# Hop 3 with its slabs 1 and 3 in another pair of PSUM banks

## The chip, the cores and the metric

One core of a Trainium2 chip runs the whole program in one launch. The metric is the device time of that launch in microseconds (us), the median of several runs. A core has five engines with an instruction queue each: TensorE (PE in the profile, with its weight loads as PEld), VectorE (DVE), ScalarE (ACT), GpSimd (POOL) and SyncE (SP, which here only issues DMAs). They wait for each other through semaphores. Matmuls write into PSUM, which has eight banks of 128 partitions by 512 float32; the other engines read the sums from there.

## The reference

The program computes two layers on a graph of 3125 nodes with 256 features and 53125 edges. The part that the change touches is the first neighbour sum of the second layer, and what runs beside it is that layer's linear attention:

```python
xn = _layernorm(x, axis=-1)
x = x + _L1_gnn_ref(xn, edge_index, ...) + _L1_mix_ref(xn[None], ...)[0]

def _gin_agg(h, src, dst, eps, n_nodes):                       # in _L1_gnn_ref
    agg = jax.ops.segment_sum(h[src], dst, num_segments=n_nodes)
    return (1.0 + eps) * h + agg
h = _gin_agg(x, src, dst, eps1, n)          # hop 3, 256 features
h = relu(relu(h @ W1a + b1a) @ W1b + b1b)
h = _gin_agg(h, src, dst, eps2, n)          # hop 4, 512 features

qkv = rmsnorm(x, g_pre) @ w_qkv              # in _L1_mix_ref
q = jax.nn.softmax(q, axis=-2) * SCALE       # within each of 4 heads of 32
k = jax.nn.softmax(k, axis=-1)               # over all nodes
out = einsum(context(k, v), q) @ w_out + b_out, then rmsnorm
```

## The kernel before

Nodes lie in 25 tiles of 128. The features of the stream are also held transposed in `AS` (called `AT`: features on the partitions, nodes along the free axis). The edges are sorted by destination, so the neighbour sum of hop 3 is written as a product with a dense matrix of edge counts. That matrix is built in the first two hops and kept in HBM as `adjacency`, in eight **slabs** of 408 destinations each. A slab has rows for all 3125 sources. It is loaded in five **pieces** of five source tiles, so there are 40 pieces, in a ring of four buffers (two in `onehot`, two in `WA`). SP loads piece i as soon as piece i-4 has been used.

`dense_products` (on PE) goes through the 40 pieces. For each piece and each half `c` of the 256 features it issues 15 matmuls of 128x408 (5 tiles, times 3 bf16 parts into which the float32 features are split: `rows`, and two in `NN`). All 75 matmuls of a slab and a half add up in one PSUM bank, `EDGE[c]`. The last matmul of a slab's half 0 counts up `slab_half`, the last of half 1 counts up `piece_used`, as each piece does.

`dense_sums` (on DVE) goes through the same 40 pieces. Behind the last piece of a slab it reads the slab's first column from a register load (`slab_base`) and adds bank `EDGE[c]` into the 408 columns of `AT` (line 1960), half 0 and then half 1, each add counting up `dense_added`. At the first piece of the next slab PE waits until the add of the same half is done (line 1076), since the slabs share the banks.

Both functions carry side work, held in two tables that are both named `beside_pieces`, from piece 3 on. On PE that is for node tile t: `queries_keys_values(t)` (line 1005, one matmul for each half, behind the 15 of the half) into a bank of the ring `TA`; ACT takes the queries out of that bank (line 1327), and DVE's `normalise_queries(t)` (lines 1876 to 1881, with an exp on ACT at line 1221 in between) makes the softmax within the heads; one piece later PE turns the result, `turn_queries(t)` (line 1012), which waits for it (`q_normed`). Piece 3, 4 and 5 carry two node tiles each, pieces 6 to 24 one each. In DVE's queue the softmax of the piece's queries stands ahead of the slab's adds. Pieces 26 and later carry the rest of the attention, whose products go to the banks `TV` by `V.next()`.

So of the eight banks, `TA` has three (ps0 to ps2), `EDGE` two, `TV` two and `PACC` one. `TV` serves the expert products ahead of hop 3 (line 987, added by DVE at line 1718; the count `pv_free` stands at `V_FFN0` when the last has been taken out), and is next used by `turn_maxima` in piece 26, the second piece of slab 5. Hop 4 (`hidden_products`, line 1145) has four feature chunks, in `EDGE` and `TV`.

Behind hop 3, DVE adds the attention's last rows (line 1930), ACT makes their squares (line 1289), and the two dense layers follow (line 1109).

Of the kernel before, what the change touches and what calls it, by code (L numbers as in the profile page):

```python
# [43 lines left out]
KC = D // P  # L44
# [28 lines left out]
SLABW = 408  # L73
# [38 lines left out]
def build(nc, a, out):  # L112
    with ExitStack() as ctx:
# [3 lines left out]
        def sem(name):  # L117
            return ctx.enter_context(nc.semaphore(name))
# [31 lines left out]
        TA, EDGE, TV, PACC = ps[0:3], ps[3:5], ps[5:7], ps[7]  # L150
# [18 lines left out]
        pv_full, pv_free = sem("pv_full"), sem("pv_free")  # L169
# [47 lines left out]
        piece_used, slab_half, dense_added = sem("piece_used"), sem("slab_half"), sem("dense_added")  # L217

        def load(eng, dst, src, s):
# [23 lines left out]
        pieces = [v.bitcast(BF16).rearrange("p (t n) -> p t n", n=SLABW) for v in (  # L243
            onehot[:, 0:8, :].rearrange("p u n -> p (u n)")[:, 0:1020],
            onehot[:, 8:16, :].rearrange("p u n -> p (u n)")[:, 0:1020], WA[:, 1024:2044], WA[:, 2048:3068])]
# [55 lines left out]
        V_GNN0, V_FFN0 = 1 + 2 * T, 1 + 3 * T  # L301
# [12 lines left out]
        def piece_of(t):  # L314

            return 3 + t // 2 if t < 6 else t

        EARLY = 9
        A_W1B = A_MIX1 + 2 * T + 2 * SLICES * HC + EARLY
# [14 lines left out]
        indeg, broken, dense_ok = sc[:, 170:171], sc[:, 171:172], sc[:, 172:173]  # L334
# [462 lines left out]
        def _(pe):  # L797
# [20 lines left out]
            for t in range(T):  # L818
                mm = nc.tensor.transpose(PACC[:, t * PARTS:(t + 1) * PARTS], VB[0:PARTS, t * P:(t + 1) * P], ident[0:PARTS, 0:PARTS])
# [3 lines left out]
            for q in range(0, T, 4):  # L823
                o = A.next()
                for t in range(q, min(q + 4, T)):
                    mm = nc.tensor.transpose(o[:, (t - q) * P:(t - q + 1) * P], dnode[:, t:t + 1].to_broadcast([P, P]), ident[:, :])
# [89 lines left out]
            for t in range(T):  # L916
# [3 lines left out]
                for c in range(KC):  # L920
                    mm = nc.tensor.transpose(o[:, c * P:(c + 1) * P], AT[:, c, t * P:(t + 1) * P], ident[:, :])
# [23 lines left out]
            for s in range(GROUPS + 2):  # L945
# [3 lines left out]
                if s >= 2:  # L949
                    normalised_transposed(1, s - 2)  # L950

                    for t in group(s - 2):
                        for c in range(KC):
                            mm = nc.tensor.matmul(PACC[:, c:c + 1], N[:, t, c * P:(c + 1) * P], valid[:, t:t + 1],
                                                  start=(t == 0 and c == 0), stop=(t == T - 1), skip_group_check=True)
# [5 lines left out]
            for c in range(KC):  # L961
                mm = nc.tensor.matmul(PACC[:, 8:8 + E0], ybar[:, c, :], wr[:, c, :], start=(c == 0), stop=(c == KC - 1))
# [3 lines left out]
            for g in range(GROUPS + 1):  # L966
                if g < GROUPS:
                    for c in range(8):
                        if g == 0 and c % 4 == 0:
                            pe.wait_ge(experts_gathered[c // 4], 16 * (KC + 1))  # L970
                        for half in range(2):
                            o = A.next()
                            n0 = g * GN + half * HALF
                            n = min(HALF, NODES - n0)
                            for k in range(KC):
                                mm = nc.tensor.matmul(o[:, 0:n], w1g[:, c // 4, k, (c % 4) * P:(c % 4 + 1) * P],  # L976
                                                      NT[:, k, n0:n0 + n], start=(k == 0), stop=(k == KC - 1))
                            mm.then_inc(pa_full, 1)
                    first_done[g] = A.n
                if g >= 1:  # L980
# [3 lines left out]
                    for t in range(GROUP):  # L984
                        o = V.next()
                        for c in range(8):
                            mm = nc.tensor.matmul(o[:, 0:D], hG[:, (g - 1) % 2, c, t * P:(t + 1) * P], w2g[:, c // 4, c % 4, :],  # L987
                                                  start=(c == 0), stop=(c == 7))
# [61 lines left out]
            for t in range(T):  # L1050
                for c in range(KC):
                    beside_pieces[piece_of(t), c if t >= 6 else t % 2].append(lambda t=t, c=c: queries_keys_values(t, c))
                if t >= 1:
                    beside_pieces[piece_of(t), 1 if t >= 6 else t % 2].append(lambda t=t: turn_queries(t - 1))
# [11 lines left out]
            def dense_products():  # L1066
                for i in range(PIECES):
                    b, q = divmod(i, GROUPS)
                    pe.wait_ge(piece_loaded[i % 4], 16 * (i // 4 + 1))
                    if b == 0:  # L1070
                        pe.wait_ge(hi_ready, q + 1)
                        pe.wait_ge(mid_ready, (q + 1) * GROUP)
                        pe.wait_ge(lo_ready, (q + 1) * GROUP)
                    for c in range(KC):
                        if q == 0 and b > 0:
                            pe.wait_ge(dense_added, KC * (b - 1) + c + 1)
                        f = slice(c * P, (c + 1) * P)
                        for n in range(GROUP):
                            t = q * GROUP + n
                            for part, rows16 in enumerate((hi16[:, t, f], both16[:, t, 0, f], both16[:, t, 1, f])):  # L1080
                                mm = nc.tensor.matmul(EDGE[c][:, 0:SLABW], rows16, pieces[i % 4][:, n, :],  # L1081
                                                      start=(t == 0 and part == 0), stop=(t == T - 1 and part == 2))
                        if c == KC - 1:
                            mm.then_inc(piece_used, 1)
                        elif q == GROUPS - 1:
                            mm.then_inc(slab_half, 1)
                        for step in beside_pieces[i, c]:
                            step()
# [9 lines left out]
            def wide(weights, src, chunks, ready, then=None):  # L1098
# [16 lines left out]
                return ends  # L1115

            dense_products()
            assert V.n == V_MIX1 and A.n == A_MIX1 + 2 * T
            product_pass(pe, 3, general=True)
# [58 lines left out]
            for t in range(T):  # L1178
                pe.wait_ge(pa_free, ends[((t + 1) * P - 1) // SL])
                mm = nc.tensor.matmul(PACC[:, t * E1:(t + 1) * E1], VB[:, t * P:(t + 1) * P], rw2, start=True, stop=True)  # L1180
            mm.then_inc(route_mm, 1)
            for e in range(E1):
# [4 lines left out]
                if e == 0:  # L1187

                    pe.wait_ge(route_sb, 2)
                    for q in range(0, T, 4):  # L1190
                        o = A.next()
                        for t in range(q, min(q + 4, T)):
                            mm = nc.tensor.transpose(o[0:E1, (t - q) * P:(t - q + 1) * P], route[5][:, t, :], ident[:, :])
# [5 lines left out]
                for t in range(T):  # L1199
                    pe.wait_ge(pa_free, ends[((t + 1) * P - 1) // SL])  # L1200
                    o = V.next()
                    for k in range(KC):
                        mm = nc.tensor.matmul(o[:, 0:D], h2[:, k, t * P:(t + 1) * P], w[:, 2, k, :], start=(k == 0), stop=(k == KC - 1))  # L1203
# [188 lines left out]
        def _(dve):  # L1392
# [536 lines left out]
            def attention_in(t):  # L1929
                nc.vector.tensor_tensor(Y[:, t, :], V.next()[:, 0:D], bout_b, ALU.add).then_inc(pv_free, 1)  # L1930

            beside_pieces = {piece_of(t): lambda t=t: normalise_queries(t) for t in range(6, T)}
            for i in range(3):
                beside_pieces[3 + i] = lambda i=i: ([over_norm(1)] if i == 0 else []) + [normalise_queries(2 * i), normalise_queries(2 * i + 1)]
# [9 lines left out]
            def dense_sums():  # L1944

                for i in range(PIECES):
                    beside_pieces.get(i, lambda: None)()
                    if i % GROUPS < GROUPS - 1:
                        continue
                    b = i // GROUPS  # L1950
                    base = dve.value_load(slab_base[0:1, b:b + 1], min_val=0, max_val=WIDE - SLABW)
                    for c in range(KC):
                        if c == 0:
                            dve.wait_ge(slab_half, b + 1)
                        else:
                            dve.wait_ge(piece_used, i + 1)
                        if b:
                            dve.wait_ge(dense_added, KC * (b - 1) + c + 1)
                        win = AT[:, c, bass.ds(base, SLABW)]
                        nc.vector.scalar_tensor_tensor(out=win, in0=EDGE[c][:, 0:SLABW], scalar=dense_ok, in1=win,  # L1960
                                                       op0=ALU.mult, op1=ALU.add).then_inc(dense_added, 1)
                dve.wait_ge(dense_added, KC * SLABS)

# [17 lines left out]
            st.settle()  # L1981
            dve.sem_inc(at_ready, 1)
            dense_sums()
            add_pass(dve, st, 3, general=True)
            dve.sem_inc(at_ready, 1)
# [155 lines left out]
```

## Time and profile before

| | us |
|---|---|
| median of 3 runs | 2993.53 (2991.62 to 2995.46) |
| the profiled execution's own time | 2993.78 |
| its span in the trace | 2992.0 |
| PE busy in the span | 2478.4 (83%) |
| DVE, ACT, POOL busy | 1299.7 (43%), 454.3 (15%), 866.6 (29%) |
| hop 3 on PE, first and last matmul of line 1081 | 1510.7 to 1829.2 |

The span is the stretch from the first to the last instruction in the trace; the time adds 1.8 us around it. Times of day in the rows below are us from the span's start.

### The profile page before, as it was taken

To read this page: it belongs to the slowest core of one execution; us is meant where nothing else is said; L and a number is where in the kernel's file an instruction comes from. 1 tells how busy PE (TensorE), PEld (TensorE's weight loads), DVE (VectorE), ACT (ScalarE), POOL (GpSimd) and SP (SyncE) were. 2 spreads that over 40 slices of the span, in tenths; PEclk is the share of its full clock that TensorE was granted. 3 is DMA by queue.
4 is the path that set the end of the run, shared out by engine and by line. 5 is a ranking of instruction groups with operands and counts; after the bars stand their busy time and mean duration, and the time that the engine had idled before them with its cause. 6 is when DMAs were issued, how large, how long until landed. Compare 5 with 4: busy or idle time off the path is not lost.

```text
span 2992.0 us, 33704 instructions
## 1 busy us (share of the span) xinstructions
PE 2478.4 (83%) x12264; PEld 1717.7 (57%) x12264; DVE 1299.7 (43%) x3544; ACT 454.3 (15%) x963; POOL 866.6 (29%) x912
## 2 busy tenths in 40 slices
PE   4577777775666666689969998999999999999999
PEld 3456655654555555567745565565555556566665
DVE  8877867756765756442572124122000003131221
ACT  0201111101000000032231103330000010413222
POOL 0177777774777777320010000110000000000000
PEclk9989999987987988779989999999999999989999
DMA  3134344343434344110022221022111100000001
GB/s 105 58 101 135 103 139 139 104 139 110 125 119 140 103 139 139 46 50 0 27 74 70 65 74 38 32 85 70 57 50 50 36 1 4 18 11 11 11 11 43
DMA packets 77650, 211.87 MB, mean 71 GB/s; under 512 B 16445, under 2 KB 33845, under 8 KB 76073
## 3 DMA queue, kind: packets, MB, share of 16 engines
q0 software_dynamic: 40800, 111.47, 12.6%
q1 hardware_dynamic: 36681, 98.17, 9.9%
q8 instruction: 103, 1.69, 0.2%
q14 instruction: 66, 0.54, 0.1%
HBM read 169.10 MB, written 40.47 MB: 70 GB/s over the span
## 4 chain that ended last, share of the span: by engine, by line
PE 63%; DVE 15%; DMA 8%; issue 6%; POOL 5%; ACT 2%; DVEq 1%; SPq 0%; ACTq 0%; POOLq 0%
PE ps L1109 16%; PE ps L1145 13%; DMA rows<-table,src_i 8%; PE ps L1081 7%; PE ps L555 6%; POOL rows L494 5%; PE ps L1203 5%; PE ps L976 3%; PE ps L987 3%; DVE onehot L674 2%; DVE NN L1666 2%; DVE NN L1654 1%; PE ps L875 1%; PE ps L1165 1%; PE ps L813 1%
## 5 line engine op out<-in xcount | busy, mean ns | idle before, releaser
L494 POOL DMA_INDIRECT rows<-table,src_i x832 | 812.5, 977 | 390.1 <-issue 303.6
L555 PE MATMUL ps<-onehot,rows 128*128 128x128 f32 x3328 | 551.4, 308 | 213.0 <-DMA rows<-table,src_i 187.8
L555 PEld LDWEIGHTS ps<-onehot,rows 128*128 128x128 f32 x3328 | 521.1, 219 | 324.2 <-issue 213.5
L1109 PE MATMUL ps<-AS,WA 128*128 128x400 f32 (+1 forms) x768 | 257.8, 498 | 12.5 <-ACT NN L1347 6.1
L875 PE MATMUL ps<-NN 128*128 128x500 bf16 x416 | 169.1, 406 | 116.2 <-DVE NN L1655 100.6
L674 DVE TENSOR_SCALAR onehot<-iota_w,rel,wgt 128x128 f32<-128x128 f32 x848 | 230.1, 361 | 2.8 <-DVE iota_w L714 1.6
L1109 PEld LDWEIGHTS ps<-AS,WA 128*128 128x128 f32 x768 | 148.0, 193 | 121.2 <-ACT NN L1347 6.7
L1109 PE MATMUL ps<-NN,WA 128*128 128x400 f32 (+1 forms) x640 | 213.5, 495 | 1.0 <-ACT rows L1360 0.7
L2079 DVE SCALAR_TENSOR_TENSOR X<-ps,WA,X 128x256 f32<-128x256 f32 x150 | 72.6, 484 | 272.1 <-PE ps L1203 272.1
L1347 ACT ACTIVATE AS<-ps,small 128x400 f32<-128x400 f32 (+1 forms) x224 | 131.2, 586 | 334.7 <-PE ps L1109 334.7
L1109 PEld LDWEIGHTS ps<-NN,WA 128*128 128x128 f32 x640 | 122.4, 192 | 88.9 <-issue 1.6
L2023 DVE SCALAR_TENSOR_TENSOR AS<-ps,small,AS 128x408 f32 x32 | 20.3, 643 | 345.9 <-PE ps L1145 345.1
L692 DVE TENSOR_TENSOR AS<-AS,ps 128x256 f32 x104 | 43.9, 422 | 278.5 <-PE ps L555 278.4
L1666 DVE TENSOR_TENSOR NN<-NN,ps 128x500 f32 x208 | 140.3, 675 | 54.5 <-issue 22.5
L1654 DVE TENSOR_SCALAR NN<-WB,AS 128x500 bf16<-128x500 f16 x416 | 151.1, 363 | 0.3
L1145 PE MATMUL ps<-WA,NN 128*128 128x408 bf16 x768 | 137.1, 336 | 0.0
L1145 PE MATMUL ps<-onehot,NN 128*128 128x408 bf16 x768 | 136.1, 336 | 0.0
L1203 PE MATMUL ps<-WA,AS 128*128 128x256 f32 x600 | 135.6, 389 | 0.0
L875 PEld LDWEIGHTS ps<-NN 128*128 128x128 bf16 x416 | 43.4, 104 | 139.8 <-DVE NN L1666 98.2
L1203 PEld LDWEIGHTS ps<-WA,AS 128*128 128x128 f32 x600 | 104.2, 192 | 31.4 <-issue 13.1
L1655 DVE TENSOR_SCALAR NN<-WB,AS 128x128 bf16<-128x128 f16 x416 | 116.5, 280 | 0.0
L793 POOL CAST rows<-WA 128x512 bf16<-128x512 f32 x5 | 4.7, 931 | 376.2 <-DVE WA L2002 376.2
(353 smaller groups left out, 3071.5 us busy)
## 6 DMA issues: line engine op xcount, KB each, us to landing
adjacency<-NN SPq DMA_DIRECT2D x8, 2550.0 KB, 9.3
onehot<-adjacency SPq DMA_DIRECT2D x40, 510.0 KB, 3.5
WA<-adjacency SPq DMA_DIRECT2D x40, 510.0 KB, 3.5
rows<-table,src_i POOLq DMA_INDIRECT x832, 2.7
table<-NN SPq DMA_DIRECT2D x10, 640.0 KB, 3.3
table<-WA SPq DMA_DIRECT2D x25, 256.0 KB, 2.0
WA<-in_experts SPq DMA_DIRECT2D x6, 768.0 KB, 4.1
X<-in_x SPq DMA_DIRECT2D x1, 3072.0 KB
```

The lines of the kernel that those rows point to most:

```text
L494: nc.gpsimd.indirect_dma_start(slot_of(h, j, k), None, table[h - 1][:, :], bass.IndirectOffsetOnAxis(index, 0)).then_inc(gathered[h - 1][( ...
L555: mm = nc.tensor.matmul(EDGE[j % 2][:, c * P:(c + 1) * P], row[:, c * P:(c + 1) * P], onehot[:, j % 2 * U + k, :], start=(k == 0 and c == ...
L674: nc.vector.tensor_scalar(onehot[:, buffer * U + k, :], iota_w[:, :], rel[:, bass.ds(c, 1)], wgt[:, bass.ds(c, 1)], ALU.is_equal, ALU.mult ...
L875: nc.tensor.matmul(build_bank(s)[:, 0:CELLS], sources_in[:, n % CELL_RING, :], cells[:, n % CELL_RING, :], start=(j == 0), stop=(j == 1)). ...
L1081: mm = nc.tensor.matmul(EDGE[c][:, 0:SLABW], rows16, pieces[i % 4][:, n, :], start=(t == 0 and part == 0), stop=(t == T - 1 and part == 2))
L1109: mm = nc.tensor.matmul(o[:, 0:n.stop - n.start], weights[:, k, c * P:(c + 1) * P], src[:, k, n], start=(k == 0), stop=(k == chunks - 1))
L1145: mm = nc.tensor.matmul(banks[c][:, 0:SLABW], hidden16(t)[:, part, f], pieces[i % 4][:, n, :], start=(t == 0 and part == 0), stop=(t == T ...
L1203: mm = nc.tensor.matmul(o[:, 0:D], h2[:, k, t * P:(t + 1) * P], w[:, 2, k, :], start=(k == 0), stop=(k == KC - 1))
L1347: nc.scalar.activation(dst[:, c, n], o[:, 0:n.stop - n.start], ACT.Relu, bias=bias[:, c:c + 1]).then_inc(pa_free, 1)
L1654: nc.vector.tensor_scalar(cells[:, n % CELL_RING, :], iota500, cell_of[:, n:n + 1], None, ALU.is_equal).then_inc(cells_ready, 1)
L1655: nc.vector.tensor_scalar(sources_in[:, n % CELL_RING, :], iota500[:, 0:P], source_in[:, n:n + 1], None, ALU.is_equal).then_inc(cells_read ...
L1666: nc.vector.tensor_tensor(part, part, build_bank(s)[:, 0:CELLS].rearrange("p (t n) -> p t n", n=SUBW), ALU.add).then_inc(slab_added, 1)
```

## The change

Slabs 1 and 3 of hop 3 accumulate in the pair `TV`, the other six in `EDGE` as before. PE's wait at the start of a slab follows from that. Slab 1 waits for `pv_free` at `V_FFN0`, slab 2 for the adds of slab 0, slab 3 for those of slab 1, slab 4 for those of slab 2, and slabs 5, 6 and 7 for those of the slab ahead of them, as before. DVE's add reads from the bank that the slab was summed in. In the changed file all lines behind the two new functions stand 6 or 8 lower.

```diff
+        def slab_banks(b):
+            return TV if b in (1, 3) else EDGE
+
+        def slab_freed_by(b):
+            return None if b < 2 else b - 2 if b < 5 else b - 1
...
                     for c in range(KC):
-                        if q == 0 and b > 0:
-                            pe.wait_ge(dense_added, KC * (b - 1) + c + 1)
+                        if q == 0 and b == 1:
+                            pe.wait_ge(pv_free, V_FFN0)
+                        if q == 0 and b > 1:
+                            pe.wait_ge(dense_added, KC * slab_freed_by(b) + c + 1)
...
-                                mm = nc.tensor.matmul(EDGE[c][:, 0:SLABW], rows16, pieces[i % 4][:, n, :],
+                                mm = nc.tensor.matmul(slab_banks(b)[c][:, 0:SLABW], rows16, pieces[i % 4][:, n, :],
...
-                        nc.vector.scalar_tensor_tensor(out=win, in0=EDGE[c][:, 0:SLABW], scalar=dense_ok, in1=win,
+                        nc.vector.scalar_tensor_tensor(out=win, in0=slab_banks(b)[c][:, 0:SLABW], scalar=dense_ok, in1=win,
```

No instruction moves; every engine has the same rows in the same order. On PE, at the end of slab 0 and the start of slab 1, the rows were these (`ps` is any PSUM bank; line 1005 is the queries' product of node tile 3, line 1012 the turn of tile 2, line 1081 the first matmul of slab 1):

```order
L1005 MATMUL ps<-WB,NN 128x384 [waits pa_free]
L1005 MATMUL ps<-WB,NN 128x384
L1012 MATMUL ps<-ident,WA 128x128 [waits pa_free,q_normed]
L1081 MATMUL ps<-onehot,rows 128x408 [waits dense_added,piece_loaded1]
L1081 MATMUL ps<-onehot,NN 128x408 x2
```

and at the same place in the changed kernel, with its own line numbers, they are:

```order
L1011 MATMUL ps<-WB,NN 128x384 [waits pa_free]
L1011 MATMUL ps<-WB,NN 128x384
L1018 MATMUL ps<-ident,WA 128x128 [waits pa_free,q_normed]
L1089 MATMUL ps<-onehot,rows 128x408 [waits pv_free,piece_loaded1]
L1089 MATMUL ps<-onehot,NN 128x408 x2
```

Only the semaphore of the first matmul's wait differs here. At the starts of slabs 2, 3 and 4 the rows read as before, and the count that `dense_added` must reach is lower by two. The adds on DVE behind the last piece of slab 1 are, in the changed kernel:

```order
L1959 TENSOR_LOAD slab_base
L1959 ISA x2
L1968 ISA [waits dense_added,slab_half]
L1968 SCALAR_TENSOR_TENSOR AS<-ps,small,AS 128x408
L1968 ISA [waits dense_added,piece_used]
L1968 SCALAR_TENSOR_TENSOR AS<-ps,small,AS 128x408
```

Nothing has moved there either, and the waits are the same; only the bank that `ps` stands for is another.

## Rows read from the trace of the kernel before

**Rows 1.** The page: chain that ended last, by engine and by line.

```profile
PE 63%; DVE 15%; DMA 8%; issue 6%; POOL 5%; ACT 2%; DVEq 1%; SPq 0%; ACTq 0%; POOLq 0%
PE ps L1109 16%; PE ps L1145 13%; DMA rows<-table,src_i 8%; PE ps L1081 7%; PE ps L555 6%; POOL rows L494 5%; PE ps L1203 5%; PE ps L976 3%; PE ps L987 3%; DVE onehot L674 2%; DVE NN L1666 2%; DVE NN L1654 1%; PE ps L875 1%; PE ps L1165 1%; PE ps L813 1%
```

**Rows 2.** Waits of PE from 1480 to 1860: us in total, times, longest.

```profile
PE ps L1081 <- DVE AS L1960: 17.2, 5, 3.5
```

**Rows 3.** Timeline of PE at slab starts: start, us, what, idle before and its releaser.

```profile
1567.08 0.27 PE L1012 MATMUL ps<-ident,WA 128*128 128x128 f32 x1
1570.75 0.33 PE L1081 MATMUL ps<-onehot,rows 128*128 128x408 bf16 x1 [3.40 <-DVE AS L1960]
...
1591.87 0.34 PE L1081 MATMUL ps<-onehot,rows 128*128 128x408 bf16 x1
...
1598.44 0.34 PE L1081 MATMUL ps<-onehot,rows 128*128 128x408 bf16 x1
...
1604.91 0.27 PE L1012 MATMUL ps<-ident,WA 128*128 128x128 f32 x1
1608.63 0.33 PE L1081 MATMUL ps<-WA,rows 128*128 128x408 bf16 x1 [3.45 <-DVE AS L1960]
...
1646.79 0.33 PE L1081 MATMUL ps<-WA,rows 128*128 128x408 bf16 x1 [3.45 <-DVE AS L1960]
...
1684.95 0.50 PE L1081 MATMUL ps<-onehot,rows 128*128 128x408 bf16 x1 [3.45 <-DVE AS L1960]
...
1723.11 0.50 PE L1081 MATMUL ps<-onehot,rows 128*128 128x408 bf16 x1 [3.46 <-DVE AS L1960]
```

**Rows 4.** Timeline of ACT and DVE at the end of slab 1.

```profile
1605.11 0.37 ACT L1327 ACTIVATE WA<-ps,small 128x128 f32<-128x128 f32 x1 [5.22 <-PE ps L1005]
...
1605.51 0.29 DVE L1876 TENSOR_REDUCE small<-WA 128x4 f32<-128x128 f32 x1 [4.76 <-ACT WA L1327]
...
1607.03 0.29 DVE L1881 TENSOR_TENSOR WA<-WA,small 128x128 f32<-128x128 f32 x1
1607.84 1.19 DVE L1960 SCALAR_TENSOR_TENSOR AS<-ps,small,AS 128x408 f32 x2 [0.51 <-issue]
```

**Rows 5.** Windows: length, busy PE, PEld, DVE, ACT, POOL, PE's granted clock, DMA.

```profile
1570.80:1575.00 4.20, 4.20 (x22) 2.49 (x23) 0.35 (x1) 0.17 (x1) 0.00 (x0) 1.00 0.01 2
1608.60:1613.00 4.40, 4.37 (x16) 2.41 (x17) 0.43 (x1) 0.00 (x0) 0.00 (x0) 0.64 0.00 0
1613.00:1643.20 30.20, 30.20 (x160) 17.23 (x158) 5.34 (x20) 4.78 (x16) 0.00 (x0) 1.00 0.23 70
1646.80:1651.20 4.40, 4.40 (x16) 2.16 (x17) 0.39 (x1) 0.00 (x0) 0.00 (x0) 0.61 0.01 4
1684.90:1689.40 4.50, 4.45 (x16) 2.30 (x17) 0.45 (x1) 0.00 (x0) 0.00 (x0) 0.62 0.00 0
2050.00:2390.00 340.00, 340.00 (x1973) 192.84 (x1972) 15.44 (x24) 0.00 (x0) 0.00 (x0) 1.00 0.17 53
```

**Rows 6.** The chain that ended last, in order of time: start, us, what.

```profile
1556.63 5.10 PE ps L1081 x15
...
1573.50 1.29 PE ps L1005 x4
1574.90 2.59 PE ps L1081 x15
...
1723.11 6.70 PE ps L1081 x30
1729.92 5.18 PE ps L1081 x30
...
1831.69 0.52 ACT WA L1289 x2
```

**Rows 7.** Timeline of DVE: the last expert sum taken out of `TV`.

```profile
1502.47 0.42 DVE L1718 TENSOR_TENSOR NN<-NN,ps 128x256 f32<-128x256 f32 x1 [0.52 <-PE ps L987]
```

**Rows 8.** DMA issues from 1560 to 1730: KB each, median us to landing.

```profile
onehot<-adjacency SPq DMA_DIRECT2D x12, 510.0 KB, 3.4
```

## The prediction

> **What bounds the kernel now.** I read the chain that ended last first. PE holds 63% of it, and the matmuls of hop 3 (line 1081) 7%: hop 3 lies on the path that sets the end, so a microsecond that PE loses there is a microsecond of the result [rows 1]. Then the waits of PE over hop 3: one waiter repeats, line 1081 for DVE's add of line 1960, five times, 17.2 us in all, 3.5 at the longest [rows 2]. The timeline of PE places them: the first matmul of slabs 1, 2, 3, 4 and 5 has idle time of 3.40 to 3.46 us ahead of it [rows 3]. Slabs 6 and 7 have none.
>
> Why the add is late is seen at the end of slab 1 [rows 4]. PE's last side work there starts at 1604.91. ACT then takes the queries (1605.11), DVE makes their softmax (1605.51 to 1607.32), reads a register (0.51 us of issue) and only at 1607.84 begins the add that frees the bank. Bank 0 had been complete for half a piece by then; its add stands behind the softmax in DVE's queue. From piece 25 on there is no softmax, hence no wait at slabs 6 and 7.
>
> Last the granted clock [rows 5]. It is 1.00, the level of 2.4 GHz, behind the first idle gap (1570.8 to 1575.0). Behind the next three it averages 0.64, 0.61 and 0.62, so for most of each stretch the engine stands at the lower level of 1.2 GHz, and then it is 1.00 again.
>
> **What the change does, part by part.**
>
> *A steady piece.* In slab 1 the piece that begins at 1591.87 is followed by one at 1598.44: 6.57 us. By the same step the next would begin at 1605.01, that is 0.10 behind the start of the turn at 1604.91. It began at 1608.63 [rows 3]. The wait therefore costs 3.62, a little over the idle time shown, since matmuls overlap.
>
> *The wait at slab 1* falls away for `pv_free`. The last expert sum left `TV` at 1502.89 [rows 7], some 64 us ahead of slab 1, so the new wait costs nothing. Slab 1 would begin at 1567.08 + 0.10 = 1567.18 instead of 1570.75: **3.57 us**. No clock was lost behind this gap, so that is all.
>
> *The waits at slabs 2, 3 and 4* now look two slabs back, at adds finished about 30 us before. Slabs 2, 3 and 4 last 38.16 us each from start to start (1608.63, 1646.79, 1684.95, 1723.11) [rows 3]. Five steady pieces are 32.85. The 5.31 between them is the wait at the end, 3.62, and 1.69 lost to the lower clock at the beginning. Without wait and dip, slab 2 starts 3.62 earlier and its own dip of 1.69 goes; likewise for slabs 3 and 4: **3 x 5.31 = 15.93 us**.
>
> *The wait at slab 5* stays, since slabs 4 and 5 share `EDGE`. Its dip stays in the sum too: the first 30 matmuls of slab 5 took 6.70 us, the next 30 5.18 [rows 6], so it is worth 1.52.
>
> *What takes the place of the wait.* PE now runs on while DVE finishes the softmax and adds, so the next thing that could be late is PE's turn of the queries one piece later. On DVE softmax and adds end 1609.03 - 1604.91 = 4.12 us after the turn begins [rows 4]. At slabs 2 to 4 the next queries reach DVE 6.57 us after the last ones did, at 1612.08 on the clock of [rows 4], and DVE is free at 1609.03: a margin of 3.0. At slab 1 it is tighter, because piece 5 carries two node tiles. Half 0 of piece 5 gives its queries at 1567.18 + 2.59 + 1.29 = 1571.06 [rows 6]; they reach DVE 0.60 later, at 1571.66, and DVE is free at 1567.08 + 4.12 = 1571.20. The softmax takes 1.81, to 1573.47, and PE wants it after half 1, at 1571.06 + 0.10 + 2.59 + 1.29 = 1575.04. It holds by 1.6. The turn of tile 3, at 1571.06, needs a softmax that ends near 1567.08 + 2.41 = 1569.49: 1.6 as well. I cost both at nothing. If that cover were gone, the two adds and the register read, 1.70 us, would come back once.
>
> *The rest costs nothing.* A piece lands 3.4 us after its issue [rows 8], and SP issues it three pieces, 19.7 us, ahead of its use; shorter slabs leave that as it is. The adds on DVE are the same instructions on another bank, and DVE is busy for 5.34 of 30.20 us in this stretch [rows 5]. What follows hop 3 waits for its last matmuls and rows: ACT's squares begin at 1831.69 and stand in the chain [rows 6], so they move forward with it.
>
> *The sum.* 3.57 + 15.93 = 19.5 us. The profiled execution took 2993.78 with a span of 2992.0, and lies 0.25 above the median, so I set the sum against the median: 2993.53 - 19.5 = **2974.0 us**.
>
> **Rule against row.** The first idle gap was as long as the others and cost no clock; the three behind it cost 1.69 each [rows 3, 5]. The Trainium skill, in TensorE: Matmul & The Clock Gate, section Why this matters for your kernels, says that idle gaps between bursts of matmuls bring the clock back to the lower level. Were every gap charged so, the sum would be 4 x 5.31 = 21.2 us and the time 2972.3; three gaps of four agree with it, the first does not, and the sum above goes by the four rows.
>
> **Both ends.** Low end of the time: the dip behind slab 5 stays away, as it did behind slab 1, and 1.5 more is gained, 2972.5. High end: only the waits go and as much clock is lost elsewhere in hop 3, for a gain of 3.57 + 3 x 3.62 = 14.4, 2979.1. Further dips behind hop 3 may fall otherwise, about one of 1.7 in either direction. The three runs shown lie within 2 us of their median. That makes 2969 to 2981.
>
> **The rivals.**
>
> *The clock does not hold without the gaps (slower).* Slabs 1 to 4 become a stream of 40 blocks of 15 matmuls with no pause. At the lower level a block takes 5.10 us, at the upper 2.59 [rows 6], 2.51 more. If the stream fell to the lower level throughout, 100 us would be lost and the time would be 3074. It turns the change into a loss from 19.5 / 2.51, or 8 blocks of the 40, on. Against it: hop 4 runs matmuls of the same shape through `EDGE` and `TV` in turn, and from 2050 to 2390 PE was busy for 340.00 of 340 us at a clock of 1.00 [rows 5]. The same page of the Trainium skill, in the section A second HAM failure mode: psum-queue depth-cycling, tells of a kernel that cycled through PSUM banks and whose clock oscillated for small idle times between groups; here the window of hop 4 speaks against it. Chance 0.02.
>
> *Something else sets the pace, and the change does nothing.* If DVE or the pieces limited hop 3, PE would only wait elsewhere, and the time stays at 2993.5. For it speaks only that DVE is what PE waited for. Against it: DVE is idle for five sixths of the stretch [rows 5], and between slab starts PE steps on at 6.57 with no idle time [rows 3]. Chance 0.03.
>
> *Part of the wait comes back at the turns, or the clock is lost all the same.* The turn at slab 1 has a margin of 1.6 only; if it fails, 1.70 returns, 2975.7; with the dips kept as well, 14.4 - 1.7 = 12.7 are left and the time is 2980.8. Chance 0.10.
>
> **How the numbers follow.** The forecast has 0.85, the rivals 0.02, 0.03 and 0.10. The predicted time is the forecast's. The range takes in the forecast with its bounds and nearly all of the third rival, and leaves out the first two, 0.05, and the tails of the others. A change under 0.2%, 6 us here, can hardly be told from none. Faster than 2987.5 are the forecast and the third rival, 0.95; the second rival gives 0.03 for the same, the first 0.02 for slower.
>
> **What would show it.** In the profile after, PE should wait for DVE's add once in hop 3, ahead of slab 5, for 3.4 to 3.5 us. Slabs 2, 3 and 4 should last 32.9 us from start to start, at a clock of 1.00, and slab 5 should start near 1703.6. PE's turn (line 1018) should show no idle time for the softmax at the start of slab 1. From hop 3's end on, the rows should stand as they were, 19.5 us earlier. I would be wrong if a wait for `q_normed` appeared at the slab starts, if the clock were below 1.00 in slabs 1 to 4, or if the stretch behind hop 3 took a few us longer than before and gave the gain back.

## The result, and the profile after

The changed kernel takes 2980.21 us in the median of five runs (2971.90 to 2981.76), the kernel before 2993.53 (2991.62 to 2996.53). The ratio is 0.9949, with a 95% interval from 0.9936 to 0.9962. That is 15.3 us less, between 11.4 and 19.2; forecast were 19.5 us and 2974.0, in a range from 2969 to 2981. The profiled execution is the fastest of the five, 2971.90 with a span of 2970.1, so a second profile of the same kernel, taken later, is read beside it: 2978.72 with a span of 2976.9.

The page of the changed kernel, first profile, the chain that ended last by engine and by line (the lines are those of [rows 1], 6 or 8 higher):

```profile
PE 64%; DVE 16%; DMA 7%; issue 6%; POOL 3%; ACT 2%; DVEq 1%; SPq 0%; ACTq 0%; POOLq 0%
PE ps L1117 16%; PE ps L1153 13%; PE ps L561 7%; DMA rows<-table,src_i 7%; PE ps L1089 7%; PE ps L1211 5%; POOL rows L500 3%; PE ps L982 3%; PE ps L993 3%; DVE NN L1674 2%; DVE onehot L680 2%; DVE NN L1662 2%; PE ps L881 1%; DVE NN L1663 1%; DVE NN L1685 1%
```

The chain is much the same: hop 3 (now line 1089) still holds 7%, and it is PE's. Its waits from 1480 to 1860, the line that answers to [rows 2]:

```profile
PE ps L1089 <- DVE AS L1968: 3.5, 1, 3.5
```

Of five waits one is left. The timeline of PE at the slab starts, to be laid beside [rows 3] (line 1018 is the turn of the queries, line 1089 the slab's first matmul):

```profile
1565.69 0.27 PE L1018 MATMUL ps<-ident,WA 128*128 128x128 f32 x1
1565.80 0.34 PE L1089 MATMUL ps<-onehot,rows 128*128 128x408 bf16 x1
...
1600.07 0.34 PE L1089 MATMUL ps<-WA,rows 128*128 128x408 bf16 x1
...
1632.94 0.34 PE L1089 MATMUL ps<-WA,rows 128*128 128x408 bf16 x1
...
1665.81 0.34 PE L1089 MATMUL ps<-onehot,rows 128*128 128x408 bf16 x1
...
1698.57 0.27 PE L1018 MATMUL ps<-ident,WA 128*128 128x128 f32 x1
1702.30 0.33 PE L1089 MATMUL ps<-onehot,rows 128*128 128x408 bf16 x1 [3.45 <-DVE AS L1968]
```

Slab 1 starts 0.11 behind the turn. Slabs 2 and 3 last 32.87 each; slab 4 lasts 36.49, since the wait ahead of slab 5 falls into it; slab 5 starts 3.73 behind its turn, as before. From slab 1 to slab 5 it is 136.50 us, where it was 152.36: 15.86 less, and 15.93 were forecast. The windows of PE between them (length, busy PE, granted clock, DMA) answer to [rows 5]:

```profile
1562.00:1595.00 33.00, 33.00 (x174) 1.00 0.25 71
1595.00:1630.00 35.00, 35.00 (x188) 1.00 0.27 84
1630.00:1665.00 35.00, 35.00 (x189) 1.00 0.25 76
1665.00:1698.00 33.00, 33.00 (x178) 1.00 0.27 80
```

The clock is 1.00 throughout, so the stream stays at the upper level without the gaps. What comes behind slab 5's start is in the chain in order of time (start, us, what), first profile:

```profile
1702.30 5.33 PE ps L1089 x30
...
1753.17 5.58 PE ps L1040 x50
...
1759.26 6.64 PE ps L1089 x30
```

and in the second profile of the same kernel:

```profile
1705.67 5.33 PE ps L1089 x30
...
1756.54 8.57 PE ps L1040 x50
...
1765.62 6.87 PE ps L1089 x30
```

The first 30 matmuls of slab 5 take 5.33 in both, against 6.70 [rows 6]: the gap of 3.45 us is there, its dip is not. Line 1040 is the attention's key sums: 25 matmuls of a single column, which the trace shows as 50, behind the first half of piece 33 (line 1034 in the kernel before). With the 30 matmuls of the slab behind it, it takes 12.22 in the first profile and 15.44 in the second. That is half of the 6.8 us between the two executions; the other half, 3.4, lies ahead of the first turn of hop 3, which begins at 1554.8 in the one and at 1558.2 in the other.

### The profile page after: what moved, and what is told of

It reads as the page before. It is cut to its first block, busy times and chain, and to the rows that moved or that the text cites. A ratio compares the mean times of both kernels' runs of the same rounds, so it can differ in the third digit from the quotient of the medians.

```text
span 2970.1 us, 33704 instructions
## 1 busy us (share of the span) xinstructions
PE 2476.5 (83%) x12264; PEld 1716.7 (58%) x12264; DVE 1300.1 (44%) x3544; ACT 454.2 (15%) x963; POOL 867.7 (29%) x912
## 4 chain that ended last, share of the span: by engine, by line
PE 64%; DVE 16%; DMA 7%; issue 6%; POOL 3%; ACT 2%; DVEq 1%; SPq 0%; ACTq 0%; POOLq 0%
PE ps L1117 16%; PE ps L1153 13%; PE ps L561 7%; DMA rows<-table,src_i 7%; PE ps L1089 7%; PE ps L1211 5%; POOL rows L500 3%; PE ps L982 3%; PE ps L993 3%; DVE NN L1674 2%; DVE onehot L680 2%; DVE NN L1662 2%; PE ps L881 1%; DVE NN L1663 1%; DVE NN L1685 1%
## 5 line engine op out<-in xcount | busy, mean ns | idle before, releaser
L1117 PEld LDWEIGHTS ps<-AS,WA 128*128 128x128 f32 x768 | 148.6, 194 | 121.3 <-ACT NN L1355 5.8
L846 PE MATMUL ps<-WA,NN 128*128 128x512 f32 x200 | 113.6, 653 | 0.0
```

The costliest lines, as they stand in the source:

```text
L1117: mm = nc.tensor.matmul(o[:, 0:n.stop - n.start], weights[:, k, c * P:(c + 1) * P], src[:, k, n], start=(k == 0), stop=(k == chunks - 1))
```

## The experiments

All times are medians, with the kernel before run beside each group on the same chip: 2995.24 for the first four, 2994.47 for the next four, 2997.33 for the last two. A gain "in the median" is one minus the ratio, times the time before.

### The changed kernel again

No edit.

> The changed kernel once more, unaltered. Its profiled execution took 2971.9 us, the other four 2979.4 to 2981.8, and the question is where those 8 to 10 us lie. Theory A (the waits were priced rightly, the rest lies outside hop 3): hop 3 again lasts some 296 to 298 us from its first to its last matmul, one wait of 3.5 us ahead of slab 5 is left, and a slower execution differs in the gathers of hops 1 and 2 or behind hop 3. Theory B (hop 3 itself has slower executions): where the profiled execution takes about 2980, hop 3 lasts 304 to 306 us, with clock dips or waits for the softmax that the first profile did not show. Times: 2972 to 2982 by either.

Measured: 2978.72 (2978.66 to 2981.07, five runs), ratio 0.9948 (0.9934 to 0.9961), 15.6 us. This profile took 2978.72, so it shows an execution of the usual length. From slab 1 to the end of slab 4 it reads the same as the first (length, busy PE, PEld, DVE, ACT, POOL, clock, DMA):

```profile
1569.20:1701.70 132.50, 132.50 (x706) 76.75 (x704) 32.77 (x113) 25.16 (x84) 0.00 (x0) 1.00 0.27 79
```

The waits were priced rightly in both. Hop 3 as a whole, from its first to its last matmul, lasts 299.3 us in this profile and 295.9 in the first, where it was 318.5: 19.2 and 22.6 less. Nearly all of the difference is the key sums, as above. Then both lose some 2 us: from hop 3's last matmul to the end of the span it is 1164.9 and 1164.7 us, and 1162.8 before. Neither theory holds as written, and 299.3 lies between their two ranges for hop 3: theory A is right on the waits, and theory B on a clock dip in hop 3, which sits in the tail that neither looked at.

### Only slab 1 in the other pair

```diff
-            return TV if b in (1, 3) else EDGE
+            return TV if b == 1 else EDGE
-            return None if b < 2 else b - 2 if b < 5 else b - 1
+            return None if b < 2 else b - 2 if b < 3 else b - 1
```

> One half of the change: only slab 1 sits in the other pair of banks, slabs 2 to 7 in the usual one. Theory A: the waits ahead of slabs 1 and 2 go, those ahead of slabs 3, 4 and 5 stay at 3.45 us each, and hop 3 gains 3.57 + 5.31 = 8.9 us, for 2984.6. Rival (the gain is not a sum over waits, but comes from the clock held over a long stretch): 2990 to 2993. Theory B: about 6 of 8.9, 2987.

Measured: 2990.97 (2988.99 to 2994.32), ratio 0.9986 (0.9977 to 0.9995), 4.2 us. Its waits of PE:

```profile
PE ps L1089 <- DVE AS L1968: 10.3, 3, 3.5
```

and the starts of slabs 3, 4 and 5 in its chain:

```profile
1636.62 4.03 PE ps L1089 x15
...
1674.37 5.26 PE ps L1089 x15
...
1713.71 7.02 PE ps L1089 x30
```

The time missed both theories: theory A had 2984.6 and theory B 2987, and 2990.97 lies in the rival's 2990 to 2993. The profile decides against the rival all the same. Two waits went and three stayed, as theory A has it, and up to the turn behind slab 5's first piece 7.6 us are gained of the 8.9; a gain that came only from a long stretch would have left 3.5 at most. Slab 4 lasts 39.34 us from start to start where it lasted 38.16 [rows 3], since the 15 matmuls of its first block, and a few behind them, ran at the lower level (5.26 against 2.59). The rest is lost as in the whole change: the key sums and the block behind them took 7.98 + 7.48 us, and from hop 3's last matmul to the end of the span it is 2.7 us more than before.

### The adds ahead of the softmax

The banks are those of the kernel before.

```diff
...
+                    if ends and i == GROUPS - 1:
+                        normalise_queries(2)
+                        slab_into_stream(0, i)
+                        normalise_queries(3)
+                    elif ends and i < T:
+                        slab_into_stream(i // GROUPS, i)
+                        beside_pieces.get(i, lambda: None)()
...
```

(`slab_into_stream` is the register read and the two adds, as they were; `ends` marks a slab's last piece. The first branch is slab 0, the second slabs 1 to 4; all other pieces keep their order.)

> The kernel before with its banks as they were; only DVE's order changes: behind the last piece of slabs 0 to 4 the two adds stand ahead of that piece's softmax (at slab 0 between the softmax of tiles 2 and 3). Theory A (PE waits because the add stands behind the softmax in DVE's queue, not for want of a bank): all five waits shrink to nothing, hop 3 gains 3.57 + 4 x 3.62 + 3 x 1.69 + 1.52 = 24.6 us, for 2968.9, less whatever the changed kernel also failed to give. Rival (one pair of banks is the limit): two or more waits of over 1 us remain at the slab starts and the time is above 2980.

Measured: 2974.25 (2973.22 to 2979.86), ratio 0.9933 (0.9920 to 0.9947), 20.1 us. Line 1081 is no longer among the waits of PE. The timeline at the end of slab 1, all engines, to be laid beside [rows 4]:

```profile
1601.89 0.64 DVE L1956 SCALAR_TENSOR_TENSOR AS<-ps,small,AS 128x408 f32 x1 [2.61 <-PE ps L1081]
...
1602.22 0.27 PE L1012 MATMUL ps<-ident,WA 128*128 128x128 f32 x1
1602.33 0.34 PE L1081 MATMUL ps<-WA,rows 128*128 128x408 bf16 x1
1602.42 0.37 ACT L1327 ACTIVATE WA<-ps,small 128x128 f32<-128x128 f32 x1 [5.22 <-PE ps L1005]
...
1602.82 0.29 DVE L1876 TENSOR_REDUCE small<-WA 128x4 f32<-128x128 f32 x1 [0.29 <-ACT WA L1327]
```

The add of half 1 runs while PE still makes the queries. The softmax begins 0.40 behind ACT, the same as in [rows 4], so it isn't delayed either. With one pair of banks all five waits are gone: they came from the order of DVE's queue. From the first turn to the last, behind slab 5's first piece, the gain is 24.3 us; forecast were 24.6. The time is 5.4 us above the 2968.9 of theory A, which had left room for what the changed kernel also failed to give, and that is where it went: the key sums and the block behind them took 8.32 + 7.12 us, and behind hop 3 another 2.5 us are lost.

### Both

The edits of the change and of the run above together.

> The changed kernel with DVE's adds ahead of the softmax as well. Theory A: the same as the new order alone, within 3 us, since no wait is left that a bank could remove; the wait ahead of slab 5 is gone and hop 3 lasts 295 us or less. Rival (a second pair still helps): 4 us or more below the new order alone.

Measured: 2973.65 (2973.15 to 2975.39), ratio 0.9929 (0.9916 to 0.9943). It is 0.6 us below the new order alone, within the forecast of 3: with the adds first, the second pair has nothing left to hide. Hop 3 lasts 295.7 us in both kernels, a little over the 295 that was forecast; the key sums and the block behind them took 8.37 + 7.09.

### A second profile of the kernel before

No edit.

> A second profile of the kernel before. Theory A2 (behind slab 5 the clock falls at places that the change shifts, and the kernel before loses less there): the 50 one-column matmuls of line 1034 and the 30 behind them take again about 13.9 us together (15.4 in the changed kernel's second profile), and the lower clock in hop 4 again lasts some 3 us (10 in all the others). Rival (the first profile was a lucky one): 15.4 and 10, and the changed kernel gives nothing back behind hop 3.

Measured: 2995.28, one run. Its chain at the key sums (line 1034) and the block behind:

```profile
1776.85 5.77 PE ps L1034 x50
...
1783.12 8.12 PE ps L1081 x30
```

and its windows of PE (length, busy, clock, DMA) at the key sums, at the start of hop 4's second slab, and behind hop 4's end, where the next dense layer begins:

```profile
1771.50:1796.50 25.00, 25.00 (x144) 0.86 0.19 53
2036.50:2061.50 25.00, 21.09 (x116) 0.93 0.30 105
2405.50:2421.50 16.00, 13.56 (x42) 1.00 0.01 2
```

The same three stretches of the changed kernel, second profile, each set at the same distance from its work:

```profile
1751.20:1776.20 25.00, 25.00 (x135) 0.80 0.14 42
2017.00:2042.00 25.00, 21.09 (x107) 0.86 0.25 76
2387.70:2403.70 16.00, 13.55 (x37) 0.89 0.01 2
```

The first profile of before was no lucky one: 13.89 us, and the clocks of the three stretches are the same in both. The changed kernel does fewer matmuls in each (135 against 144, 107 against 116, 37 against 42). So something is lost at three places, each time as a lower clock and not as a wait. Behind hop 3 the idle gaps themselves are equal in both kernels, 3.9 us ahead of hop 4's second slab and 2.4 behind its end. The waits of PE in hop 4, before and then changed:

```profile
PE ps L1145 <- DVE AS L2023: 3.9, 1, 3.9
PE ps L1109 <- DVEq L2030: 2.4, 1, 2.4
...
PE ps L1153 <- DVE AS L2031: 3.9, 1, 3.9
PE ps L1117 <- DVEq L2038: 2.4, 1, 2.4
```

### Wide key sums, in the kernel before and in the changed one

```diff
-                    nc.tensor.matmul(PACC[:, P:P + 1], kv1[0:m, 0, t, :], ones[0:m, 0:1], start=(t == 0), stop=False)
+                    nc.tensor.matmul(PACC[:, P:2 * P], kv1[0:m, 0, t, :], ones[0:m, 0:P], start=(t == 0), stop=False)
-                nc.tensor.matmul(PACC[:, P:P + 1], memk, ones[0:MEM, 0:1], start=False, stop=True).then_inc(mix_mm, 1)
+                nc.tensor.matmul(PACC[:, P:2 * P], memk, ones[0:MEM, 0:P], start=False, stop=True).then_inc(mix_mm, 1)
```

> The kernel before, with the key sums' 50 matmuls one column wide made 128 columns wide (the same sum in 128 columns, the first of which is read). Theory A2 (the clock falls in this stretch because the matmuls are so narrow): the two stretches take 5.6 + 5.2 = 10.8 us at a clock of 1.00 instead of 13.9, and the time falls by 3.1 us, to 2992. Rival (the clock falls there whatever the width, for the 7 us wait or a phase): 13.9 as before and no change in the time.

Measured: 2991.56 (2989.35 to 2996.47), ratio 0.9992 (0.9983 to 1.0001), 2.4 us, an interval that just touches no change. The stretch in its chain:

```profile
1774.34 5.77 PE ps L1034 x50
...
1780.52 5.28 PE ps L1081 x30
```

11.05 us instead of 13.9. The 128 times wider matmuls take no longer, and the dip is gone, so it hung on the narrow matmuls and not on a wait. The median alone, 2.4 us where 3.1 were forecast, would not show it.

> The changed kernel with the same wide key sums. Theory A2: 10.8 us instead of 15.4, so 4.6 us below the changed kernel, about 2974.5. Rival: 15.4 and about 2979.

Measured: 2971.07 (2967.42 to 2971.53), ratio 0.9921 (0.9907 to 0.9934), 23.7 us. It lies 7.7 to 9.1 us below the two medians of the changed kernel (other groups of runs), where 4.6 were forecast. Chain and windows, the same three stretches:

```profile
1756.26 5.77 PE ps L1040 x50
...
1762.44 5.28 PE ps L1089 x30
```

```profile
1750.90:1775.90 25.00, 25.00 (x160) 1.00 0.21 64
2012.80:2037.80 25.00, 21.09 (x115) 0.93 0.31 101
2381.80:2397.80 16.00, 13.55 (x42) 1.00 0.01 2
```

The key sums and the block behind them are near the forecast of 10.8, 11.05 us. The rest comes behind hop 3, where the clock is 0.93 and 1.00 again, as in the kernel before. Between the two wide kernels the change is worth 20.5 us.

### Both, with wide key sums

The change, the new order and the wide sums together.

> The changed kernel with DVE's adds ahead of the softmax and with the wide key sums. Theory A2: 4.6 us below the same without wide sums, about 2969. Rival: about 2974.

Measured: 2968.82 (2964.43 to 2971.33), ratio 0.9913 (0.9900 to 0.9927), 26.1 us: 4.8 below the same without wide sums (another group of runs), where 4.6 were forecast. The agreement is in part luck. From hop 3's first matmul to the end of the span the profile is 6.8 us shorter than the one without wide sums, since the dips in hop 4 are shorter too; hop 3 began 2.0 later.

### The new order and the wide sums, without the second pair

> The kernel before with its banks, DVE's adds ahead of the softmax and the wide key sums: the new order without the second pair. Theory A2: no wait at a slab start, 10.8 us for the key sums and the block behind them, and 2969, the same within 2 us as with the second pair beside it. Rival (the second pair is worth something of its own): 3 us or more above.

Measured: 2970.44 (2967.41 to 2971.58, four runs), ratio 0.9908 (0.9891 to 0.9924), 27.6 us. Its key sums and the block behind them took 5.77 + 5.28 us, and no wait for an add is left.

> The changed kernel with DVE's adds ahead of the softmax and the wide key sums once more, on the same chip as the run beside it: 2966 to 2971 by the earlier run, and within 2 us of the run beside it by theory A2.

Measured: 2968.46 (2966.45 to 2971.71, four runs), ratio 0.9908 (0.9891 to 0.9924). The two medians lie 2.0 us apart with ranges that overlap, and the ratios are equal. The second pair isn't needed; either of the two beats the kernel before and the changed one.

What lies ahead of hop 3 is the same in all kernels here, yet hop 3 begins anywhere from 1509.4 to 1516.0 us in the twelve profiles, which blurs the times. Counted from hop 3's first matmul to the end of the span, the profiles compare more sharply:

| kernel | key sums as they were, us | wide, us |
|---|---|---|
| before | 1481.3 and 1481.3 | 1477.8 |
| slab 1 alone in the other pair | 1477.8 | |
| the change | 1460.6 and 1464.2 | 1457.4 |
| the new order | 1461.0 | 1453.8 |
| both | 1460.9 | 1454.1 and 1454.0 |

Beside the new order the second pair moves this by 0.1 to 0.3 us. With wide sums the change is worth 20.4 us and the new order 24.0.

## Why the prediction was right

*The waits* went as forecast: those of slabs 1 to 4 fell away, the one of slab 5 stayed, at 3.45 us. Slab 1 to slab 5 gave 15.86 of 15.93, slab 1's start 3.56 of 3.57 (it now follows its turn by 0.11 instead of 3.67).

*The cover* held: PE has no wait for `q_normed` but the 10.1 us ahead of piece 4, which stands in both kernels. The margin of 1.6 at slab 1 was enough.

*The clock without the gaps* stayed at 1.00 over slabs 1 to 4, so the rival on the other side falls.

*The dip behind slab 5* was forecast to stay, and it went in both profiles: 5.33 against 6.70, 1.37 more gained. Up to there the change is worth 3.56 + 15.86 + 1.37 = 20.8 us.

*The step that was mis-sized* is "What follows hop 3 ... move forward with it", and with it the key sums within hop 3, both costed at nothing. Between the profiles of before and the second one after, the key sums with their block cost 15.44 - 13.89 = 1.55 more. Hop 4, from its first to its last matmul, lasts 426.8 us (1960.6 to 2387.4) instead of 425.4 (1980.1 to 2405.5), and the dense layer between it and line 1165 (now 1173) 89.2 instead of 87.6: 3.0 together. From hop 3's last matmul to hop 4's first it is 148.6 instead of 149.4, 0.8 gained. The sum is 20.8 - 1.55 - 3.0 + 0.8 = 17.05. The two later profiles differ by 2993.5 - 2976.9 = 16.6 in their spans, of which 0.5 the other way lies ahead of hop 3: 17.1. The medians give 15.3 and 15.6, with intervals that hold it. With wide key sums, where the dips are alike in both kernels, the change gives 20.4 us, nearly all of the 20.8.

*What was luck.* The range's end of 2981 had room for clock lost elsewhere in hop 3, of which 1.55 us came about, at the key sums, and for about one dip of 1.7 behind hop 3, where 3.0 came about. The median lies 0.8 us below that end, with one of the five runs above it. Two things helped that the sum did not have: the dip behind slab 5 went (1.4, in the range's low end only), and the stretch ahead of hop 4 is 0.8 shorter. One of the prediction's own signs of being wrong, a stretch behind hop 3 that takes longer and gives the gain back, came true for 2.1 us.

*Two readings* were off without touching the sum. The signs have slab 4 at 32.9 us, but the wait ahead of slab 5, which the prediction keeps, falls into slab 4. And bank 0 had been complete not for half a piece when its add began at 1607.84, but for a whole one: half 0 of the piece from 1598.44 ends 2.59 later, 6.8 us ahead of the add. The add's wait in DVE's queue is what the new order takes away.

*What stays open* is why the clock falls for longer in hop 4. It does so in every kernel with narrow key sums but the one before: hop 4 lasts 426.7 to 427.0 us there, with 12.22 us for the key sums and their block in the first profile of the change and 15.44 or 15.46 in the others. The kernel before, with 13.89, and all those with wide sums, with 11.05, have 425.3 to 425.5. The idle gaps are equal, and the time since the program's start alone doesn't decide it: the wide changed kernel and the kernel with the adds first end hop 3 within 0.1 us of each other (22.0 earlier than before), and only the second has the longer dips. The runs show that with the dip at the key sums the longer dips in hop 4 went too; how the one leads to the other, some 260 us later, they do not show.

## What to carry to other kernels

Before giving a wait another buffer, see what the late release stands behind in its engine's queue: moving two adds ahead of a softmax gave 20.1 us with the old banks; a second pair of banks, which left one of the five waits, gave 15.6; and the two together gave no more than the order alone. A second pair that also serves slab 5 was not run. A gain on TensorE's path is only safe once the clock behind it has been compared too: here some 4.6 us of 20.8 came back as dips with no instruction changed. And a stretch of very narrow matmuls is worth widening when the wider form takes the same time.

## What the runs showed of the hardware

PE was busy throughout the key sums, with matmuls of one column, and the granted clock still fell (0.80 and 0.86 in the windows above): they took up to 8.57 us, where the shortest took 5.58, and the dip reached into the block behind (6.64 to 8.12 against 5.28). With 128 columns they took 5.77 us at a clock of 1.00. An idle gap of 3.45 us did not always cost the clock: behind slab 5 it fell in the kernel before (6.70 for 30 matmuls) and not in the changed one (5.33). The Trainium skill, TensorE: Matmul & The Clock Gate, section Why this matters for your kernels, names idle gaps between bursts as what brings the clock down; four of the five gaps of before agree with it, the first and the one left in the changed kernel do not, and the key sums show a fall with no gap at all.
